# Spreading the token sort, delaying the row scatters and turning the next image sooner in a software-pipelined model block

## The reference, cut to what matters

```python
x = x + _L0_conv_ref(_gn(x), ...)      # group norm, xz = x @ W_in, depthwise 3x3 conv, then per token t:
    #   h = exp(dt_t * A) * h + (dtN_t * B_t) * x_t ;  y = einsum(h, C_t) + Dskip * x_t
    #   y = layernorm(y) * silu(z) ;  out = y @ W_out + b_out
t = t + _L1_attn_ref(_ln_t(t), ...)    # softmax(q) over features, softmax(k) over tokens, context = k.T v
t = t + _L1_ffn_ref(_ln_t(t), ...)
    logits = einsum('bsd,de->bse', x, Wg)
    top_logits, top_idx = jax.lax.top_k(logits, 2)
    top_w = softmax(top_logits)
    act = silu(einsum('bsd,edf->bsef', x, W1)) * (einsum('bsd,edf->bsef', x, W3) + b3)
    out = einsum('bse,bsef,efd->bsd', C, act, W2)      # C: top_w at the chosen experts, else 0
```

## Time and profile before

| | us |
|---|---|
| median of three runs | 3913.13 |
| lowest and highest | 3910.83, 3918.53 |
| the profiled execution | 3908.72 |
| its span, first to last instruction | 3906.9 |
| start-up before the first scan | 88.2 |
| pass of image 0, 1, 2 | 355.4, 371.1, 420.9 |
| passes of images 3 to 6 | 437.8, 444.0, 440.0, 437.7 |
| pass of image 7 | 420.0 |
| after the last scan | 490.8 |

### The profile page before, as it was taken

The page is one execution under the profiler, slowest core; times in us unless marked ns, Lnnn a source line. Parts: engine busy times, 40 slices in busy tenths (PEclk is TensorE's granted clock), DMA queues, the critical chain, the costliest instruction groups (busy, mean ns, idle before and its releaser), DMA issues.

```text
span 3906.9 us, 68984 instructions
## 1 busy us (share of the span) xinstructions
PE 3163.4 (81%) x17390; PEld 2012.8 (52%) x17390; DVE 2983.4 (76%) x5234; ACT 2553.7 (65%) x6158; POOL 2909.4 (74%) x3055
## 2 busy tenths in 40 slices
PE   5687888778889888988889887988889888776772
PEld 3233354335556555655556555655556555566662
DVE  3698989988898888878897788888898788822110
ACT  3455677457867777676867777676867777665451
POOL 1465757686769886888868897888968887966755
PEclk9788999789989998999989999999989999988896
DMA  3965656465869677886869677886869677856773
GB/s 89 221 146 129 157 124 162 120 161 137 221 177 263 153 211 197 222 221 163 233 178 244 158 208 194 231 212 162 231 185 260 157 202 195 235 150 182 241 233 109
DMA packets 420323, 730.02 MB, mean 187 GB/s; under 512 B 56203, under 2 KB 313814, under 8 KB 417750
## 3 DMA queue, kind: packets, MB, share of 16 engines
q1 hardware_dynamic: 302422, 484.13, 49.7%
q10 hardware_dynamic: 99072, 203.47, 17.0%
q0 software_dynamic: 18432, 37.93, 3.5%
HBM read 596.93 MB, written 100.07 MB: 178 GB/s over the span
## 4 chain that ended last, share of the span: by engine, by line
PE 24%; POOL 22%; issue 21%; DVE 15%; ACT 11%; DMA 4%; ACTq 2%; SPq 1%; POOLq 1%; DVEq 0%; PEldq 0%
POOL prod L698 10%; DVE state L1582 6%; PE ps_conv L901 5%; PE ps_main L967 4%; DVE ps_x L1569 3%; POOL got L821 3%; PE ps_g L1085 2%; DMA dt_rep<-dt_dram 2%; POOL rows_in L798 2%; PE ps_g L1092 2%; POOL hidden L810 2%; PE ps_y L981 2%; ACT dt_rep L1206 2%; PE ps_h L1073 2%; PE ps_x L915 1%
## 5 line engine op out<-in xcount | busy, mean ns | idle before, releaser
L698 POOL TENSOR_TENSOR prod<-state,c_rep 128x384 f32<-128x384 f32 x1536 | 1532.7, 1007 | 608.5 <-DVE state L1582 588.7
L1582 DVE TENSOR_TENSOR_SCAN state<-dt_rep,carry,ps_x 128x384 f32<-128x384 f32 x1280 | 1285.8, 1005 | 0.0
L1569 DVE TENSOR_TENSOR ps_x<-ps_x,db_rep 128x384 f32<-128x384 f32 x1536 | 852.9, 555 | 243.0 <-PE ps_x L915 223.7
L1206 ACT ACTIVATE dt_rep<-dt_rep,vecs 128x384 f32<-128x384 f32 x1536 | 917.8, 615 | 137.9 <-DMA dt_rep<-dt_dram 77.7
L915 PE MATMUL ps_x<-x_stack,copy 96*128 96x384 bf16 x1536 | 534.2, 350 | 310.8 <-DVE state L1582 306.4
L901 PE MATMUL ps_conv<-gx,w_conv 128*128 128x384 f32 x1728 | 689.6, 507 | 8.0 <-DVE parts L1599 4.6
L915 PEld LDWEIGHTS ps_x<-x_stack,copy 96*128 96x128 bf16 x1536 | 153.9, 100 | 681.6 <-DVE state L1582 493.1
L1390 ACT ACTIVATE g_sb<-ps_g,w_down 128x128 f32<-128x128 f32 x1032 | 304.2, 371 | 231.1 <-PE ps_g L1092 226.3
L901 PEld LDWEIGHTS ps_conv<-gx,w_conv 128*128 128x128 f32 x1728 | 301.1, 195 | 216.6 <-issue 129.6
L1073 PE MATMUL ps_h<-u_t,w_up 128*128 128x128 f32 x2064 | 327.5, 298 | 104.0 <-DVE silu L1799 80.0
L810 POOL TENSOR_TENSOR hidden<-g_sb,silu 128x384 f32<-128x384 f32 x344 | 343.7, 999 | 83.9 <-ACT u_out L1396 74.8
(11 more groups left out here) (256 smaller groups left out, 4958.7 us busy)
## 6 DMA issues: line engine op xcount, KB each, us to landing
dt_rep<-dt_dram SPq DMA_DIRECT2D x384, 768.0 KB
w_up<-in_w_exp ACTq DMA_DIRECT2D x344, 384.0 KB
w_down<-in_w_exp ACTq DMA_DIRECT2D x344, 193.5 KB
x_stack<-parts SPq DMA_DIRECT2D x576, 48.0 KB
u_in<-rows_in SPq DMA_DIRECT2D x344, 64.5 KB
rows_out<-u_out SPq DMA_DIRECT2D x344, 64.0 KB
dt_dram<-dt SPq DMA_DIRECT2D x192, 96.0 KB
qv<-in_x SPq DMA_DIRECT2D x48, 192.0 KB
```

What stands on the lines that cost most here:

```text
L698: pool.tensor_tensor(prod[:, k % HS, :], state[:, k % HS, :], c_rep[:, c % 2, :], ALU.mult).then_inc(s_prod.sem, 1)
L1206: act.activation(dt_rep[:, g % XS, q, :], dt_rep[:, g % XS, q, :], ACT.Exp, scale=decay_rate).then_inc(s_decay.sem, 1)
L1569: dve.tensor_tensor(x_n, x_n, db_rep[:, c % 2, :], ALU.mult).then_inc(s_inflow.sem, 1)
L1582: dve.tensor_tensor_scan(state[:, k % HS, :], dt_rep[:, g % XS, q, :], ps_x[k % XB][:, 0:T], init, ALU.mult, ALU.add).then_inc(s_state.sem, 1)
```

## The change

Five things are changed.

- All six transposes of the next image use the shared banks (EARLY 6) in steps 123 to 129 instead of 124 to 131; five of them go to `ps_g`, one to `ps_h`. The group norm comes two steps sooner (slots 4, 7, 10 of chunk 4), and the first nine taps begin in slot 12 instead of 14.
- The second half of the top-2 choice is four steps later, the nine sort steps are spread over steps 143 to 164 instead of 136 to 144, and `route(4)` and `route(5)` are at 136 and 138.
- Four small DVE instructions are folded into others, so DVE_POST falls from 30 to 26.
- The scatters of a pass begin at step 168 and go on to slot 47 of the next pass (before 146 to slot 22). So `u_tok` stays in use longer: the attention input is loaded into and normalised in `k_tok`, SP waits before this load for the sort alone, and ACT waits for the scatters before it writes `ek0` to `u_tok`.
- In the end program ENDED, SPREAD and RESUMED are 16, 22 and 22 steps later and T_END is 460 instead of 438.

```diff
-EARLY = 4
-T_TURN = (124, 129, 129, 131, 128, 130)
+EARLY = 6
+T_TURN = (123, 124, 125, 127, 128, 129)
 T_XLOAD = 114
-T_GM, T_GV, T_GN = 6, 9, 12
-LATE_TAPS = ((14, 14, 15, 15, 16, 16, 17, 17, 18), (22, 22, 23, 24, 24, 25, 25, 26, 27))
+T_GM, T_GV, T_GN = 4, 7, 10
+LATE_TAPS = ((12, 13, 13, 14, 15, 16, 16, 17, 18), (22, 22, 23, 24, 24, 25, 25, 26, 27))
...
-T_TOP = ((119, 0, 9), (126, 9, 14), (127, 14, 18))
-T_PLACE = ((120, 0, 3), (121, 3, 6), (122, 6, 9), (128, 9, 12), (129, 12, 15), (130, 15, 18))
-T_CHOSEN, T_RANK, T_SORT = 132, 135, 136
+T_TOP = ((119, 0, 9), (130, 9, 14), (131, 14, 18))
+T_PLACE = ((120, 0, 3), (121, 3, 6), (122, 6, 9), (132, 9, 12), (133, 12, 15), (134, 15, 18))
+T_CHOSEN, T_RANK = (136, 138), 141
+T_SORT = (143, 146, 149, 152, 154, 156, 158, 161, 164)
...
-T_SCATTER = tuple(146 + 15 * k // 8 for k in range(NT)) + tuple(183 + 15 * k // 8 for k in range(NT))
-T_SCATTER_LAST = tuple(146 + k for k in range(NT)) + tuple(165 + k for k in range(NT))
-
-
-T_HOLD, SOONEST = T_GATHER[0] - 1, 264
-ENDED, SPREAD, RESUMED = 34, T_SCATTER_LAST[0], T_SCATTER_LAST[-1] + 8
+T_SCATTER = tuple(168 + 2 * k for k in range(NT)) + tuple(208 + 15 * k // 8 for k in range(NT))
+T_SCATTER_LAST = tuple(T_SCATTER[0] + k for k in range(NT)) + tuple(T_SCATTER[0] + 19 + k for k in range(NT))
+
+
+ENDED, SPREAD, RESUMED = 50, T_SCATTER_LAST[0], T_SCATTER_LAST[-1] + 8
+T_HOLD, SOONEST = T_GATHER[0] - 1, T_W + SC - (RESUMED - 3)
 SLOWLY = 70
 T_END = T_SUM[-1] + STORE + 1 + SC - SOONEST
-DVE_POST, POOL_POST = 30, 19
+DVE_POST, POOL_POST = 26, 19
...
-                    due(sp, s_scatter, m, 0)
+                    due(sp, s_sorted, m, 0)
                     apart()
                     if m == 0:
                         sp.wait_ge(s_init.sem, 2 * 16 * len(INIT))
-                    sp.dma_start(u_tok, image_rows(t1_dram, m).rearrange("p (k d) -> p k d", d=D)).then_inc(s_t1in.sem, 16)
+                    sp.dma_start(k_tok, image_rows(t1_dram, m).rearrange("p (k d) -> p k d", d=D)).then_inc(s_t1in.sem, 16)
...
-                        act.wait_ge(*full(m, "xnT5"))
+                        due(act, s_scatter, m, 0)
...
-                    normalise(m, 0, t - T_NORM, u_tok, u_tok)
+                    normalise(m, 0, t - T_NORM, k_tok, k_tok)
...
-                    tie(m, dve.tensor_copy(place[:, :, :], where[:, :, :]))
                     for k in range(TOP):
-                        ins = dve.tensor_tensor(chosen[k], place[:, :, k].unsqueeze(1).broadcast_to([P, NE, NT]),
+                        ins = dve.tensor_tensor(chosen[k], where[:, :, k].unsqueeze(1).broadcast_to([P, NE, NT]),
                                                 iota[:, 0:NE].unsqueeze(2).broadcast_to([P, NE, NT]), ALU.is_equal)
...
-                    tie(m, dve.tensor_scalar(gw[:, 1, :], gw[:, 0, :], 1.0, None, ALU.add))
-                    tie(m, dve.reciprocal(gw[:, 2, :], gw[:, 1, :]))
+                    tie(m, dve.tensor_scalar(gw[:, 1, :], gw[:, 0, :], 2.0, 2.0, ALU.mult, ALU.add))
                 if n == 7:
-                    tie(m, dve.tensor_scalar(u_weight, gw[:, 2, :], 0.5, None, ALU.mult))
+                    tie(m, dve.reciprocal(u_weight, gw[:, 1, :]))
...
-                tie(m, dve.tensor_scalar(tally[:, 3, :], counts[:, NE * NT:NE * NT + NE], 1.0 / P, None, ALU.mult))
-                tie(m, dve.tensor_tensor(picked[:, :, :], tally[:, 3, :].unsqueeze(2).broadcast_to([P, NE, NT]),
-                                         iota[:, 0:NT].unsqueeze(1).broadcast_to([P, NE, NT]), ALU.is_gt))
+                tie(m, dve.scalar_tensor_tensor(out=picked[:, :, :], in0=counts[:, NE * NT:NE * NT + NE].unsqueeze(2).broadcast_to([P, NE, NT]),
+                                                scalar=1.0 / P, in1=iota[:, 0:NT].unsqueeze(1).broadcast_to([P, NE, NT]),
+                                                op0=ALU.mult, op1=ALU.is_gt))
...
-                tie(m, dve.tensor_scalar(tally[:, 3, :], tally[:, 3, :], float(P), None, ALU.mult))
-
-                tie(m, dve.tensor_tensor(rank[:, :, :], counts[:, 0:NE * NT].rearrange("p (e t) -> p e t", e=NE),
-                                         tally[:, 3, :].unsqueeze(2).broadcast_to([P, NE, NT]), ALU.add))
+                tie(m, dve.scalar_tensor_tensor(out=rank[:, :, :], in0=tally[:, 3, :].unsqueeze(2).broadcast_to([P, NE, NT]), scalar=float(P),
+                                                in1=counts[:, 0:NE * NT].rearrange("p (e t) -> p e t", e=NE),
+                                                op0=ALU.mult, op1=ALU.add))
```

26 lines of the change are left out of this document (13 added, 13 removed).

## The result

The changed kernel takes 3958.86 us (median of 4 runs, 3949.3 to 3964.08), the kernel before 3913.61 us in the same comparison. The ratio is 1.0111, 95% interval 1.0088 to 1.0135, some 43 us more. The forecast was 3891 us, 22 us less; the range, up to 3932, does not hold the time.

What follows compares the result with a forecast made beforehand. No engine was taken to bound the kernel throughout; the bound changes hands inside a pass. The terms -42 - 13 + 29 + 4 + 0.5 = -21.5 us, from 3913.13, gave 3891 us, range 3860 to 3932.

Steps and rivals of the forecast that it cites:

- sort strewn, turn, fused instructions: Steps 120 to 167: less DVE work, 6.5 us gained in each of five passes, less in the others; 42 us faster.
- statistics before step 28: Before step 28: fewer scatters let POOL's attention-input statistics come 2.4 us sooner a pass; 13 us faster.
- scatters in steps 29 to 61: Steps 29 to 61: 11 more scatters delay POOL's subtraction at step 56, 5.8 us a pass; 29 us slower.
- end program: End program: 11 scatters of image 6 delay image 7's attention; 4 us slower, 0 to 8.
- start: Start of the kernel: five transposes share one bank; 0.5 us slower.
- The rival of the strewn steps: Steps 120 to 167: strewn sort steps pay in full and delay PE, the 42 shrink to about 21; 3912.6 us, chance 0.13.
- the third rival: Steps 25 to 61: POOL becomes the bound, folds wait for products, 15 us a pass; 3938 us, chance 0.17.
- The three rivals: POOL catches up, 3863 us, 0.2; strewn steps pay in full, 3912.6, 0.13; POOL bounds steps 25 to 61, 3938, 0.17.

Runs made afterwards that it cites:

- B and D: Kernel before with only the turn (with group norm and first taps) and the four fused DVE instructions changed: 0.9918, 32 us faster.
- C: The strewing (sort steps, later top-2 choice and rank product) on top of all other parts of the change: about 25 us slower.
- strew_sort: Changed kernel with the top-2 choice and rank product back at their old steps, the nine sort steps still strewn: 1.0044 of the kernel before.
- bd_0: Kernel before with the turn and the fused instructions, the third transpose in the other shared bank as before the change: 0.9925 of the kernel before.

## Why the prediction was wrong

**The parts, each with its term,** in us, measured between the two profiled executions (+53.6; some 4 lie in other steps):

| term | predicted | measured |
|---|---|---|
| sort strewn, turn, fused instructions | -42 | +2 in steps 128 to 191 (by the ratios: B and D -32, C +25) |
| statistics before step 28 | -13 | -13.3 in steps 0 to 31 of images 2 to 7 |
| scatters in steps 29 to 61 | +29 (5.8 a pass) | +42 (8.4 a pass) in steps 32 to 63 of images 3 to 7 |
| end program | +4 (0 to 8) | +12.2 |
| start | +0.5 | +6.6, of it some 2 by the turn |

**Two steps failed, of about the same size: the rank product, put at nothing, and the price of the late scatters.** Forecast and result lie 65 us apart. By the ratios 25 of them are the rank product. The late scatters were put at -13 + 29 + 4 = +20 us; they came at +45 alone and +51 on top of the turn and the fused instructions, 25 to 31 more. And strewing, turn and fused instructions were to bring 42; the last two brought 32, the strewn sort nothing. With the rank product left at 135 the kernel is still 17 us slower than before (strew_sort), so the rank alone does not explain the miss.

**The rank product** is the term that the prediction did not have. The part on the strewing counted what each DVE instruction brings and takes, and of PE it said only that it "has 70.9 us in these steps and keeps it". `T_RANK`, from 135 to 141, is in the diff and in none of my sentences. Its work on PE is 0.7 us and its sum over the stretch does not change, which is why a count of busy time cannot see it. The order matters: at 135 PE waits for DVE, at 141 DVE waits for PE. It cost 25 us. I had weighed PE's wait for a shared bank for the turn (2 us, nothing for the sum) and not for the other claimant of the same banks.

**What was right there.** DVE's work in steps 128 to 159 came out at 71.2 us (71.7 predicted), and with the rank where it was these steps take 79.2 us (78). But the gain was put down to the wrong edit. The kernel without strewing has it already, at 80.8 us, and strewing the sort adds nothing to it: what left steps 128 to 143 came back behind them (6.9 us out, 5.3 and 1.7 in). Of the four fused instructions the largest, 1.73 us in the earlier trace rows, mostly returned in the instruction it was fused into: that one took 0.31 us before and takes 1.88 in the unstrewn kernel, in the place of 1.73 + 0.31. Image 0 gained 9.1 us (1.5 predicted, 0 to 3): DVE's idle time there fell from 11.4 to 5.1 us when the taps were spread.

**The rival of the strewn steps** said that they pay in full, for the shared port. The traces have both sides. Without strewing one fused sort instruction (L1710) lasts 1.88 us beside a POOL instruction of 1.81; strewn, the same instruction (L1711) has no such neighbour and takes 0.31:

```profile
1998.99 1.88 DVE L1710 SCALAR_TENSOR_TENSOR big_k<-tally,big_k 128x144 f32<-128x144 f32 x1
```

```profile
1998.89 1.81 POOL L704 TENSOR_TENSOR dt<-dt,dt_tmp 128x768 f32<-128x768 f32 x1
```

```profile
2021.07 0.31 DVE L1711 SCALAR_TENSOR_TENSOR big_k<-tally,big_k 128x144 f32<-128x144 f32 x1
```

Others became longer; the weights' product took 0.19 us bunched and 1.00 strewn. DVE's sum over steps 128 to 167 of image 4 is 87.3 us without strewing and 86.7 with the sort strewn. The Trainium skill, "SBUF — State Buffer", section "SBUF: two separate sides", has whoever starts first hold the shared port pair for the whole instruction, where the VectorE instruction has two inputs in SBUF, as this one has, or runs in a 2-port mode. The rows agree with it: 1.88 us beside the 1.81 of POOL. They do not make the rival right: it left 21 of the 42 us, the turn and the fused instructions brought 32 without any strewing, and the strewn sort brought nothing.

**The scatters** went in kind as the third rival described: folds waited for products and PE stood with the scans. But the idle time was used in part, as the forecast had it: of 13 us added, 8.2 came out in steps 32 to 63 of images 3 to 6, and POOL's idle time in steps 29 to 61 fell from 13.9 to 9.0 us. The term was 5.8 us a pass, at the softmax (the middle of 5.1 and 6.9 would be 6.0); it measured 8.2, at the fold of step 51. The rival put it at 15 us. My reading of the earlier trace rows was right (no room behind step 42), but I followed the lateness to the subtraction at step 56, past the folds on the way, each of which can stop PE. The gain before step 28 came as predicted, 13.3 us for 13; in image 4 DVE's wait for ACT there fell from the 4.6 us of the earlier trace rows to 2.3.

**The end** was priced at 13.8 us of scatters less 9.7 of idle time. The idle time was not used: POOL's waits there end with DMAs and with DVE, in the middle of a chain, and a scatter in front of a gather only delays what the next wait hangs on. The full 12 came (9.5 of it at the subtraction: 89.7 us after the last scan, before 80.2), which is near the 13.8 and outside the 0 to 8 that I gave the term. That the idle time is lost in this way is argued from the lines; no run isolates it.

**The start** was priced at 0.5. Transposes into one bank wait for ACT's read-out of the one before, two of them in a row here, 0.58 us each, and the last begins at 36.24 us, before at 33.51:

```profile
31.42 0.90 PE L886 MATMUL ps_g<-eye,qv 128*128 128x128 f32 x3 [0.58 <-ACT gx L1198]
32.91 0.90 PE L886 MATMUL ps_g<-eye,qv 128*128 128x128 f32 x3 [0.58 <-ACT gx L1198]
...
36.24 0.90 PE L886 MATMUL ps_g<-eye,qv 128*128 128x128 f32 x3
```

In the ten other kernels with this turn the first scan starts at 90.6 to 91.9 us, in an eleventh at 94.5; in the seven with the old one at 87.9 to 91.0. So the turn costs some 2 us, and the rest of the 6.6 lies within the scatter of single executions. That these waits are the 2 us is not shown: with one transpose in the other bank (bd_0) the start was no shorter.

**The chances.** The three rivals were taken as alternatives, and two of them, one on DVE's side and one on POOL's, could be true together; with the rank the sum then leaves the range. The upper end lay "part of the way" to a rival of 3938 with a chance of 0.17; it should have reached it. Even so it would not have held 3959.

## What to carry to other kernels

When a table moves an instruction, ask on each engine what that engine waits for just before and just behind the new place. Where it waited for the others, an instruction and its wait are free; where the others wait for it, a matmul of 0.7 us with a bank to wait for cost about 4 us a pass. An engine at 89% of a stretch may be full: look for what stands behind it in in-order lists (here every fourth step's fold). Added work there cost 0.6 to 1.25 us for each of its microseconds. Before crediting a gain to one edit of a bundle, ask what the others give without it: here two small edits alone, 0.9918, beat the whole.
